# Post-norm layer on one core: in the setup, clip logarithms of chunks 1 and 2 on GpSimd, the third weight's scale and Wo's maxima sooner, ScalarE's queue reordered

## The chip, the cores and the metric
One core of one Trainium2 chip. The metric is the device time of one execution in microseconds (us).

## What is computed
The inputs are x (8 sequences of 2048 tokens, 256 features), four 256x256 matrices Wr, Wk, Wv, Wo, a decay and an ln weight of 256 values, and a feed-forward layer with 1024 hidden features. The reference, cut to what matters:

```
r = sigmoid(x @ Wr.T);  k = x @ Wk.T;  v = x @ Wv.T
dec = sigmoid(decay);   log_decay = log(clip(dec, 1e-7))
scale = exp(t * log_decay)                       # t = 0 .. 2047
cum = cumsum(k * v / clip(scale, 1e-10), axis=1)
y = rmsnorm(r * (cum * scale), ln_w)
x1 = layernorm(x + y @ Wo.T)
h = gelu(x1 @ (alpha1 * sign(w1)).T + b1)        # alpha = mean |w| of each row
out = layernorm(x1 + h @ (alpha2 * sign(w2)).T + b2)
```

## The kernel before
The tokens are cut into 32 chunks of 512 (4 to a sequence). A chunk passes through these steps: x is split into a high and a low half in fp16 (`xh` on ScalarE, `xl` on VectorE); TensorE forms k, v and r (`R`); VectorE multiplies them (`kvs`), where k is multiplied with a table `clip_g`; VectorE scans over time with the decay and multiplies by the gate (`scans`, result `y`); ScalarE forms the gate (`r_gates`) and the squares of y (`ysq`); GpSimd adds the squares and takes powers (`ysqs`, `y_scale`, `root_rms`); y is split (`yh`, `yl`), TensorE multiplies with Wo (`O`), VectorE adds the residual and normalizes (`residual1`, `ustats`, `norm1`). Then the first feed-forward layer (`F1`, `gelu`), the split of its result (`hh`, `hl`), the second one (`F2`), and the second norm.

The scan needs no exponentials, except where the reference's `clip(scale, 1e-10)` takes hold. That is what `clip_g` is for: for each feature and each time step in the sequence it holds min(1, exp(t * log_decay + 23.03)). It has 2048 columns, a part of 512 for each of the chunks 0 to 3 of a sequence, and is built once, in the setup. The parts 0 and 1 are built by `clip_logs(n)` on VectorE (t * log_decay, then the minimum with -23.03; two instructions, one for each half of the features) and `clip_table(n)` on ScalarE (exponential with a bias of 23.03, two instructions). The parts 2 and 3 are built by `clip_excess(n)` (a Relu) and `clip_table(n)` (exponential with scale -1), both on ScalarE.

Each engine works through a queue written by hand: a straight prologue, which fills the pipeline with chunks 0 to 3 and prepares the weights, and a loop over the chunks. Semaphores order the engines. The weights of k, v and r (numbered 0, 1, 2 in this order) are prepared one after the other: VectorE takes the maximum (`proj_maximum`), TensorE spreads it over the partitions (`sum_wmax`), VectorE makes the scale (`proj_scale`), ScalarE rounds the scaled matrix (`proj_split_hi`), VectorE makes its low half (`proj_split_lo`). The halved `w_inv` of the third one releases GpSimd's `unscales(0, 0)`, without which the first `kvs` can't start. Wo is prepared by `wo_maxima` (line 1133), `wo_scale`, `wo_split_hi`, `wo_split_lo`. `take_xbound(1, 1)` on VectorE (line 890) reads the sum that TensorE has formed from the squares of chunk 1's x (`xsq`, `sum_xbound`) and releases GpSimd's `scales(1, 1)` and `unscales(1, 1)`, and through them ScalarE's `xh(1)`. `signs` turns w1 and w2 into their signs, and the SP queue transposes these by DMA. `x1h(0)` (line 673) is the split of the first chunk's normalized rows, which TensorE has transposed in `T1(0)`; `x1l(0)` (line 992) is its low half; the first `F1` waits for it.

Of the kernel before, what the change touches and what calls it, by code (L numbers as in the profile page):

```python
# [27 lines left out]
def postln_layer_kernel(nc, x, Wr, Wk, Wv, Wo, decay, ln_w, w1, b1, w2, b2, out):  # L28
    fp32, fp16, bf16 = mybir.dt.float32, mybir.dt.float16, mybir.dt.bfloat16
    ALU, ACT, AX = mybir.AluOpType, mybir.ActivationFunctionType, mybir.AxisListType  # L30
# [23 lines left out]
    with ctx:  # L54
# [3 lines left out]
        def sem(name):  # L58
            return ctx.enter_context(nc.semaphore(name))
# [136 lines left out]
        s_w1T, s_w2T = sem("w1T_s"), sem("w2T_s")  # L196
        s_winv, s_wscl, s_proj_hi, s_alpha = sem("winv_s"), sem("wscl_s"), sem("proj_hi_s"), sem("alpha_s")
        s_clip, s_exp, s_nlog, s_excess = sem("clip_s"), sem("exp_s"), sem("neg_log_s"), sem("clip_excess_s")
        s_lnw, s_wo_hi = sem("lnw_s"), sem("wo_hi_s")
        s_passed = [sem("passed_pool_s"), sem("passed_dve_s")]  # L200

# [433 lines left out]
        def _(act):  # L635
# [100 lines left out]

            def clip_table(n):

                if n < 2:
                    act.wait_ge(s_clip, DC * n + DC)  # L740
                else:
                    act.wait_ge(s_excess, DC * n - DC)
                for dc in range(DC):
                    part = clip_g[:, dc, n * CH:(n + 1) * CH]
                    if n < 2:
                        nc.scalar.activation(part, part, ACT.Exp, bias=log_clip[:, :]).then_inc(s_exp, 1)
                    else:
                        nc.scalar.activation(part, part, ACT.Exp, scale=-1.0).then_inc(s_exp, 1)
# [33 lines left out]
            def prologue():  # L782
                xh(0, 0)
                proj_split_hi(0)
                clip_table(0)
                proj_split_hi(1)
                clip_table(1)
                proj_split_hi(2)
                xsq(1, 0, 1)
                clip_excess(2)  # L790
                r_gates(0, 0, (0,))
                clip_table(2)
                xh(1, 1, slot=1)
                signs(w1_in, w1_sgn, s_w1_in, s_sgn)
                xsq(2, 0, 2)
                r_gates(0, 0, (1,))
                wo_split_hi()
                ysq(0, (0,))
                ysq(0, (1,))
                r_gates(1, 1, (0,))  # L800
                clip_excess(3)
                yh(0)
                xh(2, 2, slot=2)
                clip_table(3)
                nc.scalar.activation(warm[:, :], ones_col[:, :], ACT.Gelu)
                r_gates(1, 1, (1,))
                signs(w2_in, w2_sgn, s_w2_in, s_sgn2)
                act.wait_ge(s_ysqs, 1)
                ysq(1, (0,), y=y_second)
                xsq(3, 0, 3, looped=True)  # L810
                alphas1()
                r_gates(2, 2, (0,))
                act.wait_ge(s_sgn2, 1)
                alphas2()
                x1h(0, 1)
                ysq(1, (1,), y=y_second)
                r_gates(2, 2, (1,))
                act.wait_ge(s_ready, 1)
                gelu(0, range(0, 1))
                yh(1, y_second)  # L820
                gelu(0, range(1, 2))
                act.wait_ge(s_ready, 2)
                hh(0, pairs[0])
                gelu(0, range(2, 4))
                hh(0, pairs[1])
                gelu(0, range(4, 6))
                hh(0, pairs[2])
                gelu(0, range(6, 8))
                x1h_rows(1, 1)
                hh(0, pairs[3])  # L830
                xh_rows(3, 3)
                take_alpha2_row()
# [47 lines left out]
        def _(dve):  # L880
# [239 lines left out]
            proj_scale(1)  # L1120
            proj_split_lo(0)
            proj_maximum(2)
            clip_logs(1)
            proj_split_lo(1)
            proj_scale(2)
            dve.wait_ge(s_wscl, 3)
            nc.vector.tensor_scalar_mul(w_inv[:, 2:3], w_inv[:, 2:3], 0.5).then_inc(s_winv, 1)
            proj_split_lo(2)

            def wo_maxima():  # L1130
                dve.wait_ge(s_wo_in, 16)
                dve.wait_ge(s_rows, 1)
                nc.vector.tensor_reduce(w_max[:, 3:4], wo_in[:, :, :], AX.XY, ALU.max,
                                        apply_absolute_value=True).then_inc(s_wmax, 1)
                nc.vector.tensor_reduce(w_max[:, 4:5], lnw_c[:, :], AX.X, ALU.max,
                                        apply_absolute_value=True).then_inc(s_wmax, 1)

            def wo_scale():

# [35 lines left out]

            def prologue():
                dve.wait_ge(s_exp, DC)
                kvs(0, 0, 0)
                take_xbound(1, 1)
                wo_maxima()  # L1180
                scans(0, 0, 0)
                xl(1, 1, slot=1)
                kvs(0, 0, 1)
# [92 lines left out]
        def _(pool):  # L1276
# [122 lines left out]
            nc.gpsimd.tensor_copy(fold[:, 1:TT, :], fold[:, 0:1, :].to_broadcast([P, TT - 1, P // TT]))  # L1399
            pool.wait_ge(s_setup_a, 2)  # L1400
            nc.gpsimd.tensor_scalar(neg_log[:, :], dec_c[:, 1, :], -1.0, 1.0, ALU.mult, ALU.mult).then_inc(s_nlog, 1)
            pool.wait_ge(s_winv, 1)
            unscales(0, 0)
            def prologue():
                scales(1, 1)
                unscales(1, 1)
                ysqs(0)
                y_scale(0)
                y_unscale(0)
# [70 lines left out]
```

## Time and profile before

| what | value |
|---|---|
| median of 3 runs | 821.02 us (820.99 to 821.21) |
| the profiled execution | 821.11 us, span 819.3 us |
| TensorE busy | 798.8 us, 97% of the span |
| VectorE busy | 771.3 us, 94% |
| ScalarE busy | 679.9 us, 83% |
| GpSimd busy | 295.3 us, 36% |

The span runs from the first to the last instruction. In the profile PE is TensorE, DVE is VectorE, ACT is ScalarE, POOL is GpSimd and SP is the queue that issues most DMAs. A busy share is an average over the whole span; the setup is its first 60 us or so.

### The profile page before, as it was taken

The page shows a single profiled execution, that of the slowest core. Times are in us where ns is not written, and L with a number is a line of the kernel's source. Part 1 is how long each engine was busy: PE and PEld are TensorE (multiplying, and loading weights), DVE is VectorE, ACT ScalarE, POOL GpSimd, SP SyncE. Part 2 cuts the span into 40 slices and gives each one's busy share as a digit, 9 for nine tenths or more (in the row PEclk, how much of TensorE's full clock was granted, in tenths as well). Part 3 has the DMA queues.
Part 4 walks back from the last instruction along what each step waited for, and adds up shares of the span by engine and source line. Part 5 has one row for each costly group of instructions (what it writes and reads, how often), then busy time and mean ns, then how long its engine had stood idle before and what let it go on. Part 6 is the DMA issues. An engine that isn't in the chain of part 4 may idle for free.

```text
span 819.3 us, 16575 instructions
## 1 busy us (share of the span) xinstructions
PE 798.8 (97%) x5174; PEld 505.7 (62%) x5174; DVE 771.3 (94%) x1472; ACT 679.9 (83%) x973; POOL 295.3 (36%) x572
## 2 busy tenths in 40 slices
PE   6989999999999999999999999999999999999986
PEld 4555666656666656666656666655666665666654
DVE  7998999999999999999999999999999999999887
ACT  7987888888888888888888888888888888887775
POOL 3343323344223344333344333344333334332344
PEclk9999999999999999999999999999999999999999
DMA  8513553434553434553434454444454344444313
GB/s 261 99 27 78 129 125 84 110 94 102 128 128 86 115 81 105 125 128 92 113 79 109 118 128 100 105 89 106 112 128 105 100 97 104 106 102 104 78 26 104
DMA packets 168286, 86.27 MB, mean 105 GB/s; under 512 B 128572, under 2 KB 163912, under 8 KB 168264
## 3 DMA queue, kind: packets, MB, share of 16 engines
q1 hardware_dynamic: 147288, 52.97, 27.5%
q0 software_dynamic: 4608, 16.78, 10.4%
q10 hardware_dynamic: 16368, 16.25, 5.6%
q8 instruction: 11, 0.18, 0.1%
q14 instruction: 11, 0.09, 0.0%
HBM read 20.45 MB, written 16.78 MB: 45 GB/s over the span
## 4 chain that ended last, share of the span: by engine, by line
PE 88%; DVE 4%; POOL 2%; ACT 2%; issue 2%; DMA 0%; SPq 0%; POOLq 0%; DVEq 0%; ACTq 0%
PE ps_r L375 28%; PE ps_o L496 26%; PE ps_f L446 19%; PE ps_r L446 6%; PE ps_o L401 6%; PE ps_o L406 3%; DVE hid_lo L1008 1%; DVE u L959 1%; ACT hid L678 1%; DVE u_st L967 0%; PE ps_s L383 0%; DMA x_in<-in_L_attn_x_dram 0%; POOL root L1322 0%; POOL y_sqs L1310 0%; DVE state L923 0%
## 5 line engine op out<-in xcount | busy, mean ns | idle before, releaser
L496 PE MATMUL ps_o<-w2T,hid_hi 128*128 128x256 f16 x992 | 218.9, 273 | 3.4 <-DVE hid_lo L1008 3.0
L496 PE MATMUL ps_o<-w2T,hid_lo 128*128 128x256 f16 x992 | 218.8, 272 | 0.0
L375 PE MATMUL ps_r<-x_t,proj_hi 128*128 128x512 f16 x768 | 197.1, 379 | 1.2 <-issue 0.7
L446 PE MATMUL ps_f<-x_t,w1T 128*128 128x512 f16 x768 | 181.7, 379 | 1.6 <-DVE x_t L992 1.3
L678 ACT ACTIVATE hid<-ps_f,rows_c,f_scale 128x512 f32<-128x512 f32 x192 | 145.2, 774 | 42.2 <-PE ps_f L446 37.1
L1008 DVE SCALAR_TENSOR_TENSOR hid_lo<-hid,hid_scale,hid_hi 128x1024 f16<-128x1024 f32 (+1 forms) x136 | 160.3, 1222 | 0.9 <-POOL hid_hi L1343 0.6
L1310 POOL TENSOR_TENSOR y_sqs<-y_sq 128x512 f32<-128x512 f32 x32 | 46.7, 1459 | 309.6 <-ACT y_sq L653 309.6
L375 PEld LDWEIGHTS ps_r<-x_t,proj_hi 128*128 128x128 f16 x768 | 74.7, 98 | 91.3 <-issue 2.8
L713 ACT ACTIVATE hid_hi<-hid,hid_scale 128x2048 f16<-128x2048 f32 (+2 forms) x72 | 127.9, 1778 | 3.2
L446 PEld LDWEIGHTS ps_f<-x_t,w1T 128*128 128x128 f16 x768 | 74.9, 98 | 79.7 <-issue 1.6
L375 PE MATMUL ps_r<-x_t,proj_lo 128*128 128x512 f16 x384 | 114.2, 379 | 0.2 <-DVE proj_lo L1084 0.2
L496 PEld LDWEIGHTS ps_o<-w2T,hid_hi 128*128 128x128 f16 x992 | 97.0, 98 | 20.2 <-DVE hid_lo L1008 5.9
L496 PEld LDWEIGHTS ps_o<-w2T,hid_lo 128*128 128x128 f16 x992 | 97.1, 98 | 14.4
L647 ACT ACTIVATE r_tanh<-ps_r,x_scl 128x512 f32<-128x512 f32 x64 | 43.9, 686 | 32.6 <-PE ps_r L375 29.4
L653 ACT ACTIVATE y_sq<-y 128x512 f32<-128x512 f32 x62 | 39.1, 630 | 37.0 <-ACT res L707 15.9
L446 PE MATMUL ps_r<-x_t,w1T 128*128 128x512 f16 x256 | 69.6, 378 | 0.0
L707 ACT ACTIVATE res<-res,z_shift,z_rstd 128x256 f32<-128x256 f32 x126 | 65.1, 589 | 4.8 <-POOL z_shift L1356 2.6
L1322 POOL TENSOR_TENSOR root<-ms,neg_half 128x4 f32<-128x4 f32 x32 | 32.8, 1024 | 93.0 <-DVE ms L949 93.0
L375 PEld LDWEIGHTS ps_r<-x_t,proj_lo 128*128 128x128 f16 x384 | 37.5, 98 | 45.7 <-DVE proj_lo L1084 0.9
L696 ACT ACTIVATE res<-u,u_shift,u_rstd 128x256 f32<-128x256 f32 x120 | 61.9, 588 | 1.7 <-POOL u_shift L1338 1.7
L923 DVE TENSOR_TENSOR_SCAN state<-decay_f,state,kvg 128x512 f32<-128x512 f32 x48 | 61.5, 1281 | 0.8
L401 PE MATMUL ps_o<-wo_lo,y_hi 128*128 128x256 f16 x248 | 59.2, 272 | 0.0
(191 smaller groups left out, 1332.2 us busy)
## 6 DMA issues: line engine op xcount, KB each, us to landing
x_in<-in_L_attn_x_dram SPq DMA_DIRECT2D x32, 512.0 KB, 4.1
res<-b_row POOLq DMA_DIRECT2D x32, 512.0 KB, 4.5
out_dram<-res ACTq DMA_DIRECT2D x31, 512.0 KB, 2.9
w_in<-in_L_ffn_w_dram SPq DMA_DIRECT2D x2, 1024.0 KB, 8.8
x_t<-x_st SPq DMA_TRANSPOSE x59, 3.7
b_row<-in_L_ffn_b_dram SPq DMA_DIRECT2D x1, 512.0 KB, 12.7
proj_in<-in_L_attn_Wk_dram SPq DMA_DIRECT2D x1, 256.0 KB, 3.8
proj_in<-in_L_attn_Wv_dram SPq DMA_DIRECT2D x1, 256.0 KB, 4.1
```

The lines of the kernel that those rows point to most:

```text
L375: last = nc.tensor.matmul(ps_r[:, m, :], w[:, m, dc, ec * P:(ec + 1) * P], xx[:, :, dc, :], start=(n == 0), stop=(n == 3 * DC - 1))
L401: nc.tensor.matmul(dst[:, tt, :], y_hi[:, dc, tt * P:(tt + 1) * P], w[:, dc, :], start=(dc == 0 and n == 0), stop=False)
L446: last = nc.tensor.matmul(f1_bank[hc % NF], w1T[:, hc, dc, :], xx[:, :, dc, :], start=(dc == 0 and n == 0), stop=(dc == DC - 1 and n == 1))
L496: last = nc.tensor.matmul(o_tok[:, tt, :], hh[:, hc, tt * P:(tt + 1) * P], w2T[:, :, hc, :], start=(hc == 0 and n == 0), stop=(hc == HC - ...
L647: nc.scalar.activation(r_tanh[:, ec, :], ps_r[:, 2, :], ACT.Tanh, scale=x_scl[:, j, 4:5]).then_inc(s_r, 1)
L678: nc.scalar.activation(hid[:, hc, :], f1_bank[hc % NF], ACT.Gelu, bias=b1c[:, hc:hc + 1], scale=f1_scale[:, hc:hc + 1]).then_inc(s_gelu, 1)
L696: nc.scalar.activation(res[j][:, tt, :], u[:, tt, :], ACT.Identity, bias=u_shift[:, tt:tt + 1], scale=u_rstd[:, tt:tt + 1]).then_inc(s_x1, 1)
L707: nc.scalar.activation(res[j][:, tt, :], res[j][:, tt, :], ACT.Identity, bias=z_shift[:, tt:tt + 1], scale=z_rstd[:, tt:tt + 1]).then_inc( ...
L713: nc.scalar.activation(hid_hi[:, part, :], hid[:, part, :], ACT.Copy, scale=hid_scale[:, :]).then_inc(s_hh, part.stop - part.start)
L923: nc.vector.tensor_tensor_scan(state[j % 2][:, ec, :], decay_f[:, ec, :], kvg[:, ec, :], first, ALU.mult, ALU.add).then_inc(s_scan, 1)
L1008: nc.vector.scalar_tensor_tensor(out=hid_lo[:, part, :], in0=hid[:, part, :], scalar=hid_scale[:, :], in1=hid_hi[:, part, :], op0=ALU.mult ...
L1310: nc.gpsimd.tensor_tensor(y_sqs[:, :], y_sq[:, 0, :], y_sq[:, 1, :], ALU.add).then_inc(s_ysqs, 1)
```

## The change
Five edits, all in the setup:
- the clip logarithms of chunks 1 and 2 are formed on GpSimd (`clip_logs_pool(1)` ahead of `unscales(0, 0)`, `clip_logs_pool(2)` behind `unscales(1, 1)`), with a semaphore of their own; `clip_logs(1)` leaves VectorE and `clip_excess(2)` leaves ScalarE, and `clip_table(2)` becomes an exponential with a bias;
- so the third weight's `proj_scale(2)` stands sooner in VectorE's queue;
- Wo's maxima stand ahead of `proj_split_lo(2)` and no longer behind `take_xbound(1, 1)`;
- `take_xbound(1, 1)` is put between k and v of the first `kvs`;
- in ScalarE's queue `clip_table(1)` and `clip_table(2)` are moved later, `clip_excess(3)` later as well (behind `xh(2)`), `xsq(2)` behind `wo_split_hi` and the first `ysq` ahead of it, behind `signs`.

```diff
@@ clip_table, ScalarE
-                if n < 2:
-                    act.wait_ge(s_clip, DC * n + DC)
+                if n == 0:
+                    act.wait_ge(s_clip, DC)
+                elif n < 3:
+                    act.wait_ge(s_clip_pool, DC * n)
                 else:
-                    act.wait_ge(s_excess, DC * n - DC)
+                    act.wait_ge(s_excess, DC)
                 for dc in range(DC):
                     part = clip_g[:, dc, n * CH:(n + 1) * CH]
-                    if n < 2:
+                    if n < 3:
                         nc.scalar.activation(part, part, ACT.Exp, bias=log_clip[:, :]).then_inc(s_exp, 1)
                     else:
                         nc.scalar.activation(part, part, ACT.Exp, scale=-1.0).then_inc(s_exp, 1)
@@ prologue, ScalarE
                 proj_split_hi(0)
                 clip_table(0)
                 proj_split_hi(1)
-                clip_table(1)
                 proj_split_hi(2)
                 xsq(1, 0, 1)
-                clip_excess(2)
                 r_gates(0, 0, (0,))
-                clip_table(2)
+                clip_table(1)
                 xh(1, 1, slot=1)
                 signs(w1_in, w1_sgn, s_w1_in, s_sgn)
-                xsq(2, 0, 2)
+                ysq(0, (0,))
                 r_gates(0, 0, (1,))
                 wo_split_hi()
-                ysq(0, (0,))
+                xsq(2, 0, 2)
                 ysq(0, (1,))
                 r_gates(1, 1, (0,))
-                clip_excess(3)
+                clip_table(2)
                 yh(0)
                 xh(2, 2, slot=2)
+                clip_excess(3)
                 clip_table(3)
@@ setup, VectorE
             proj_maximum(2)
-            clip_logs(1)
             proj_split_lo(1)
             proj_scale(2)
             dve.wait_ge(s_wscl, 3)
             nc.vector.tensor_scalar_mul(w_inv[:, 2:3], w_inv[:, 2:3], 0.5).then_inc(s_winv, 1)
-            proj_split_lo(2)
...
+            wo_maxima()
+            proj_split_lo(2)
@@ prologue, VectorE
                 dve.wait_ge(s_exp, DC)
-                kvs(0, 0, 0)
-                take_xbound(1, 1)
-                wo_maxima()
+                kvs(0, 0, 0, between=lambda: take_xbound(1, 1))
                 scans(0, 0, 0)
@@ setup and prologue, GpSimd
+            def clip_logs_pool(n):
+
+                pool.wait_ge(s_setup_a, 2)
+                part = slice(n * CH, (n + 1) * CH)
+                for dc in range(DC):
+                    nc.gpsimd.tensor_scalar(clip_g[:, dc, part], steps[:, part], dec_c[:, 1, dc:dc + 1], -LOG_CLIP,
+                                            ALU.mult, ALU.min).then_inc(s_clip_pool, 1)
+
+            clip_logs_pool(1)
             pool.wait_ge(s_winv, 1)
             unscales(0, 0)
             def prologue():
                 scales(1, 1)
                 unscales(1, 1)
+                clip_logs_pool(2)
                 ysqs(0)
```

## Rows read from the trace of the kernel before
**Rows 1.** Busy time by stretch; columns: length, each engine's busy us (instructions), clock, DMA.
```profile
0.00:63.10 63.10, 51.97 (x296) 30.67 (x296) 54.97 (x121) 53.69 (x92) 22.32 (x51) 1.00 0.49 126
63.10:774.80 711.70, 711.66 (x4636) 452.36 (x4637) 682.29 (x1276) 598.03 (x838) 253.25 (x490) 1.00 0.44 106
774.80:819.30 44.50, 35.14 (x244) 22.64 (x241) 34.09 (x77) 28.20 (x44) 19.71 (x31) 0.97 0.24 65
```
**Rows 2.** The chain that ended last, 12 to 19 us; columns: start, us, what.
```profile
12.17 0.80 DVE clip_g L1107 x2
12.99 0.94 ACT clip_g L746 x2
...
14.23 0.67 ACT proj_hi L726
...
18.03 1.24 DVE state L923
```
**Rows 3.** ScalarE in order of time, 17 to 44 us; columns: start, us, what.
```profile
17.25 0.67 ACT L647 ACTIVATE r_tanh<-ps_r,x_scl 128x512 f32<-128x512 f32 x1
17.82 1.14 ACT L748 ACTIVATE clip_g<-clip_g 128x512 f32<-128x512 f32 x2
...
23.73 0.84 ACT L754 ACTIVATE wo_hi<-ps_f,lnw_scl 128x256 f16<-128x256 f32 x2 [0.35 <-DVE lnw_scl L1146]
24.45 0.63 ACT L653 ACTIVATE y_sq<-y 128x512 f32<-128x512 f32 x1
...
25.52 0.63 ACT L653 ACTIVATE y_sq<-y 128x512 f32<-128x512 f32 x1 [0.34 <-DVE y L926]
...
26.81 1.51 ACT L734 ACTIVATE clip_g<-steps,neg_log_clip,neg_log 128x512 f32<-128x512 f32 x2
28.30 1.15 ACT L658 ACTIVATE y_hi<-y,y_roots 128x1024 f16<-128x1024 f32 x1
...
30.36 1.14 ACT L748 ACTIVATE clip_g<-clip_g 128x512 f32<-128x512 f32 x2
...
42.69 0.19 ACT L773 ACTIVATION_READ_ACCUMULATOR w_in<-w_in 128x1 f32 x1
43.12 1.02 ACT L673 ACTIVATE x_t<-ps_f 128x1024 f16<-128x1024 f32 x1 [0.24 <-PE ps_f L336]
```
**Rows 4.** VectorE in order of time, four places between 12 and 30 us.
```profile
12.87 0.74 DVE L1084 SCALAR_TENSOR_TENSOR proj_lo<-ps_o,w_scl,proj_hi 128x512 f16<-128x512 f32 x1
13.54 0.15 DVE L1079 TENSOR_SCALAR w_inv<-ps_s 128x1 f32<-128x1 f32 x1
13.72 0.16 DVE L1080 RECIPROCAL w_scl<-w_inv 128x1 f32<-128x1 f32 x1
...
17.18 0.68 DVE L1133 TENSOR_REDUCE w_max<-wo_in 128x1 f32<-128x512 f32 x1
...
28.46 1.30 DVE L923 TENSOR_TENSOR_SCAN state<-decay_f,state,kvg 128x512 f32<-128x512 f32 x1
```
**Rows 5.** GpSimd in order of time, three places between 4 and 30 us.
```profile
4.04 1.37 POOL L1395 TENSOR_SCALAR decay_f<-steps,dec_c 128x512 f32<-128x512 f32 x2 [0.43 <-DVE dec_c L1092]
...
27.56 0.71 POOL L1300 TENSOR_TENSOR y_roots<-y_q,halves 128x2 f32<-128x2 f32 x1
...
29.11 0.64 POOL L1285 TENSOR_TENSOR x_root<-x_scl 128x1 f32<-128x1 f32 x1
```
**Rows 6.** TensorE in order of time: the third product, and the first layer's.
```profile
15.00 1.02 PE L375 MATMUL ps_r<-x_t,proj_hi 128*128 128x512 f16 x4 [0.72 <-issue]
15.86 0.59 PE L375 MATMUL ps_r<-x_t,proj_lo 128*128 128x512 f16 x2
...
45.55 1.89 PE L446 MATMUL ps_f<-x_t,w1T 128*128 128x512 f16 x8 [0.56 <-DVE x_t L992]
```
**Rows 7.** Wo's load: its issue, and from the DMA view, median us to landing.
```profile
4.32 0.51 SPq L278 DMA_DIRECT2D wo_in<-in_L_attn_Wo_dram  x1
...
wo_in<-in_L_attn_Wo_dram SPq DMA_DIRECT2D x1, 256.0 KB, 5.7
```

More of the change, by code:

```diff
@@ L198, in postln_layer_kernel @@
         s_clip, s_exp, s_nlog, s_excess = sem("clip_s"), sem("exp_s"), sem("neg_log_s"), sem("clip_excess_s")
+        s_clip_pool = sem("clip_pool_s")
         s_lnw, s_wo_hi = sem("lnw_s"), sem("wo_hi_s")
```

## The prediction
> **What bounds the kernel now.** I read the busy table by stretches first [rows 1]. Of the span of 819.3 us the middle, from 63.1 to 774.8, has TensorE busy for 711.66 of 711.70 us at a granted clock of 1.00: there TensorE sets the pace and nothing in it can be shortened by a setup edit. The first 63.1 us have 51.97 us of TensorE, so 11.1 us of holes. All that this change touches lies there. A microsecond that the setup gives back moves the whole middle and the end by the same amount, if the state at 63.1 is only shifted.
>
> Then the chain of waits [rows 2]. In the setup it runs from VectorE's clip logarithms of chunk 1 (12.17, two of them, 0.80) to ScalarE's exponentials of them (12.99), because ScalarE has `clip_table(1)` in its queue ahead of the third weight's rounding (14.23), and then through ScalarE's `clip_excess(2)` to the first scan on VectorE (18.03).
>
> Last, ScalarE's order in time [rows 3]. The reader is to see two places. It waits for the scale of Wo (0.35 us before 23.73) and for TensorE ahead of `x1h(0)` (0.24 before 43.12). And from `yh(0)` at 28.30 to the end of the second alpha pass (42.69 + 0.19 = 42.88) it doesn't wait at all. It is full there, so what is put into this stretch is paid one for one, and what other engines gain ahead of it can't pass through it.
>
> **Part 1: the early shift.** Times below are those of before plus shifts.
> - VectorE no longer computes `clip_logs(1)`: 0.78 us (12.87 less 12.09) [rows 4]. `proj_split_lo(1)` starts at 12.09, and `w_inv` of the third weight comes not at 13.54 but at 12.09 + 0.67 = 12.76. The factor 0.67 is 13.54 less 12.87.
> - ScalarE no longer has `clip_table(1)` in front of `proj_split_hi(2)` (12.99 to 14.23) [rows 2]. The third weight's rounding waits for its scale only: the reciprocal starts 0.18 after `w_inv` and takes 0.16 [rows 4], with a hand-over of 0.04, so 12.76 + 0.38 = 13.14. That is 1.09 sooner.
> - TensorE's third product follows it from 15.00 to 13.91, and ends at 14.77 + 0.59 = 15.36, where before it was 16.45 [rows 6]. It needs the low half of this weight at 14.77: VectorE has `w_inv` halved by 13.3, Wo's maxima take 0.6 (0.68 from start to end [rows 4]) and about 0.1 for the small one, and Wo has been in SBUF since 10.0 (issued at 4.32, 5.7 to landing [rows 7]), so `proj_split_lo(2)` runs 13.95 to 14.69. It just fits. Moving `wo_maxima()` thus costs nothing here.
> - `kvs(0,0,0)`: k at 14.62 to 15.36. The bound of chunk 1 is read now between k and v. TensorE's sum for it stands right behind the third product, about 15.20 + 0.17, so VectorE reads it at 15.43 and v starts at 15.50. Without it v would start at 15.47. Price 0.03. Behind v the same read and Wo's maxima are gone.
> - First scan: v ends at 16.25, the gate (ScalarE at 15.45, since `clip_excess(2)` no longer stands before it) at 16.12, so the scan starts at 16.29 in place of 18.03 [rows 2]; y ends at 18.24.
> - ScalarE next: gate 15.45, `clip_table(1)` at 16.02 (0.57 later, as 17.25 to 17.82), 1.24 for it (12.99 to 14.23), `xh(1)` at 17.26 to 18.35. `xl(1)` on VectorE is at 18.38 where it was 20.00: **the shift is now 1.62 us**.
> - It stays so to `yh(0)`. VectorE's queue is the same from there on. ScalarE's moved `xsq(2)` now stands after the rounding of Wo. The factors of Wo come 1.62 sooner, ScalarE starts on Wo at 22.11, adds 0.72 (23.73 to 24.45) and 1.04 for the square, and is free at 23.87; the second `y` ends at about the same time (its square waited for it and started at 25.52 [rows 3]; less 1.62 that is 23.90). A tie: no loss, or 0.1. Then the sum of the bounds, GpSimd's `y_roots` (27.56 to 28.27 before [rows 5]) and `yh(0)` go from 28.30 to 26.68. `clip_table(2)`, 1.24, now fills 25.2 to 26.4, in the shadow of GpSimd's root where `clip_excess(3)` lay from 26.81 to 28.30.
>
> **Part 2: where it is given back.** `clip_excess(3)` is moved behind `xh(2)`, into the full stretch, and `clip_table(3)` waits for it directly. `yh(0)` 26.68, plus 2.06 for `yh` and `xh` (28.30 to 30.36), gives 28.74; plus 1.51 for the two excesses, and a hand-over of 0.02 to 0.1, gives 30.27 to 30.35 for `clip_table(3)`. Before it was 30.36. **Of 1.62 us there is 0.01 to 0.09 left on ScalarE.** TensorE and VectorE do arrive 1.62 sooner at `T1(0)`, but `x1h(0)` then waits for ScalarE. It used to wait 0.24 for TensorE after 42.88 (the next instruction may start 0.1 before the end of an accumulator read, so 0.34 of room). It starts at 42.78 less 0.01 to 0.09, that is 42.69 to 42.77, in place of 43.12: gain 0.35 to 0.43. I take 0.4.
>
> From there on everything hangs on `x1h(0)`: `x1l(0)` on VectorE and the first layer's product on TensorE, which waited for it until 45.55 [rows 6], then VectorE almost without a hole up to 63. So 0.4 arrives at 63.1, and the middle carries it to the end. The execution profiled took 821.11; the sum is 821.11 less 0.4, and the median of the runs shown is 0.09 lower, which gives 820.6.
>
> **Part 3: GpSimd.** It gets two pairs of 128x512 passes. The nearest row is the decay table of the same shape, 1.37 us for two [rows 5]. The first pair runs from 8.62 to 10.0, and what is queued behind it, `unscales(0,0)`, waits for `w_inv` until about 13.3 anyway: cover 3.3 us. The second stands after `unscales(1,1)` and before `ysqs(0)`, which is due at 24.7; it can start at 18.5 at the latest reckoning and end at 20: cover 4.7 us. Cost nothing, and if a pass took three times as long, the first pair would still end by 12.8. Its consumers come at 16.02 and 25.2.
>
> What the trace shows against it: GpSimd's `x_root`, one element per partition, takes 0.64 us (29.11 to 29.75), nearly as long as a pass over 512, and ends with VectorE's scan (28.46 to 29.76) [rows 4, 5]. So one of the two can stop the other. The Trainium skill ("SBUF — State Buffer", section "Who interferes with whom") makes it a lock: a VectorE instruction with two SBUF inputs and a GpSimd instruction that reads SBUF exclude each other for the whole instruction, and the first to start wins. By that rule, the row agrees, but it shows GpSimd as the loser only; this change could make VectorE the loser. By my schedule neither pair meets a scan or a y: the sum by the row and by the rule is the same unless the order slips.
>
> **The rivals.**
> - *A, the whole shift arrives*: ScalarE's full stretch gives way (a hole in it that I don't see, or the excess costs nothing there). The shift of 1.62 reaches `x1h(0)` as far as TensorE allows, 821.02 less 1.62 = 819.4. For it: TensorE and VectorE really are early. Against: [rows 3] has no hole between 28.30 and 42.88.
> - *B, slower: GpSimd's second pair takes the way of VectorE's first y.* `x_root` and the scan are both due at 16.3. If GpSimd gets in ahead of the y at 17.5 with both passes, y, `xl(1)`, and all up to `yh(0)` come 1.2 to 1.4 later than in part 1. Nothing absorbs it on the way, ScalarE is full behind it. Gain 0.4 less 1.3: 0.9 slower, 821.9. It decides once VectorE loses more than 0.4. Against: the y is in VectorE's queue before the passes can be, since two small operations precede them.
> - *C, the early shift is smaller than 1.62*: each 0.1 lost there is 0.1 lost at the end. Bounds: if only the 1.09 of the third weight comes through, the end is 0.1 slower, 821.2. The tie on ScalarE and the fit of the low half point this way.
> - *D, nothing is changed in the end*: the first layer waits for something else than `x1h(0)` (the transposed weights, say), 821.0. Their sign pass on ScalarE, from which they are transposed, comes 1.6 sooner as well, and in the trace the first layer waits for `x1l(0)` alone, 0.56 [rows 6].
>
> **How the numbers follow.** The forecast (gain of 0.2 to 0.6) 0.55, A and what lies between it and the forecast 0.12, B 0.08, C 0.15, D 0.10. The bound between a change and none is 0.2%, 1.64 us, so 819.38 to 822.66: the forecast, C, D and B all lie inside; A sits on the lower edge. Faster 0.08 (A with a bit more), same 0.89, slower 0.03 (B twice). The range: 819.7 holds all but the far half of A, 821.6 all but most of B.
>
> **What would show it.** The third weight's rounding near 13.1, the first scan near 16.3, `yh(0)` near 26.7: part 1. `clip_table(3)` within 0.1 of 30.3, no wait of ScalarE for TensorE ahead of `x1h(0)`, which starts near 42.7: part 2. GpSimd's four new passes 0.69 each, and no VectorE scan or y longer than 1.3 and 0.7: part 3. If `x1h(0)` starts near 41.5, A holds. If `xl(1)` starts after 19, B. The prediction is wrong if the middle stretch is no longer 711.7 us, for then the state at 63.1 is not merely shifted.

## The result and the profile after

The changed kernel takes 823.39 us (median of ten runs, 822.62 to 824.35), and the kernel before, run beside it, 821.11 (ten runs, 820.93 to 822.1). The ratio is 1.0027 with a 95% interval of 1.0019 to 1.0036: **slower by 0.27%, some 2.3 us**. Forecast were 820.6 and no measurable change. The profiled execution of the changed kernel took 824.16, with a span of 822.4.

The busy time of the changed kernel by stretch, cut at the same places of the program as [rows 1] (columns as there):

```profile
0.00:62.70 62.70, 51.93 (x294) 30.22 (x295) 52.54 (x117) 51.04 (x85) 31.51 (x55) 0.97 0.52 126
62.70:776.00 713.30, 712.01 (x4640) 452.16 (x4638) 682.30 (x1275) 598.94 (x841) 255.43 (x490) 1.00 0.44 105
776.00:822.40 46.40, 35.80 (x246) 22.71 (x243) 36.24 (x80) 28.69 (x46) 20.64 (x31) 0.95 0.28 78
```

Against [rows 1] three things stand out. TensorE's granted clock in the first stretch is 0.97 where it was 1.00. GpSimd (the fifth busy column) has 31.51 us there where it had 22.32. And the last stretch is 1.9 us longer, which no line of the diff touches. Both cuts are made by eye, so the middle's 713.3 and 711.7 can't be set against each other; GpSimd's sums of `y_sq` (`y_sqs` in the profile), one per chunk, tell the lateness better. The third, just behind the setup, is at 65.84 before and at 67.16 now (1.3 late); from the seventh to the last but one they are 1.38 to 1.42 late, in short 1.39; the last one (777.17 before) starts at 780.57, 3.4 late.

**The setup up to 27 us.** ScalarE and VectorE of the changed kernel in order of time:

```profile
13.18 0.69 ACT L727 ACTIVATE proj_hi<-ps_f,w_scl 128x512 f16<-128x512 f32 x1 [1.47 <-DVE w_scl L1082]
...
26.79 1.15 ACT L659 ACTIVATE y_hi<-y,y_roots 128x1024 f16<-128x1024 f32 x1 [0.19 <-POOL y_roots L1301]
...
28.63 1.11 ACT L640 ACTIVATE x_t<-ps_f,x_scl 128x1024 f16<-128x1024 f32 x1 [0.69 <-POOL x_scl L1281]
29.64 1.51 ACT L735 ACTIVATE clip_g<-steps,neg_log_clip,neg_log 128x512 f32<-128x512 f32 x2
31.18 1.15 ACT L751 ACTIVATE clip_g<-clip_g 128x512 f32<-128x512 f32 x2
...
43.62 1.00 ACT L674 ACTIVATE x_t<-ps_f 128x1024 f16<-128x1024 f32 x1
```
```profile
16.36 1.22 DVE L925 TENSOR_TENSOR_SCAN state<-decay_f,kvg 128x512 f32<-128x512 f32 x1
18.46 1.28 DVE L885 SCALAR_TENSOR_TENSOR x_t<-ps_o,x_scl,x_t 128x1024 f16<-128x1024 f32 x1 [0.15 <-ACT x_t L640]
...
26.92 1.28 DVE L925 TENSOR_TENSOR_SCAN state<-decay_f,state,kvg 128x512 f32<-128x512 f32 x1
```

Part 1 came to pass: the third weight's rounding at 13.18 (forecast 13.14), the first scan at 16.36 (16.29), `xl(1)` at 18.46 (18.38), `yh(0)` at 26.79 (26.68). Then `xh(2)`, the row at 28.63, waits 0.69 for a scale that GpSimd makes, and this makes `clip_table(3)` start at 31.18 (forecast 30.3) and `x1h(0)` at 43.62 (forecast 42.7, before 43.12 [rows 3]).

GpSimd of the changed kernel shows both the new passes and the late scale:

```profile
8.71 4.09 POOL L1409 TENSOR_SCALAR clip_g<-steps,dec_c 128x512 f32<-128x512 f32 x2
...
26.98 1.56 POOL L1281 TENSOR_TENSOR x_scl<-x_scl,neg_half 128x1 f32<-128x1 f32 x1
```

A pair of clip logarithms takes 4.09, three times the decay table's 1.37 [rows 5]. And `x_scl`, one element per partition, takes 1.56: it starts at 26.98, just inside VectorE's scan (26.92 to 28.20), and ends at 28.54, behind it. In e1, the changed kernel once more, the two lie almost the same way, and neither stops the other:

```profile
26.86 1.31 DVE L925 TENSOR_TENSOR_SCAN state<-decay_f,state,kvg 128x512 f32<-128x512 f32 x1
```
```profile
26.91 0.54 POOL L1281 TENSOR_TENSOR x_scl<-x_scl,neg_half 128x1 f32<-128x1 f32 x1
```

Here `x_scl` is done in 0.54, wholly inside the scan. It starts 0.05 behind the scan, and in after 0.06, so the profile's start times alone don't tell which of the two gets its turn.

**TensorE at 43 us** is where, in this trace, 0.5 us of lateness becomes 1.3. TensorE of the changed kernel in order of time:

```profile
43.07 0.17 PE L481 MATMUL ps_s<-w_max,ones 128*128 128x1 bf16 x1
45.29 0.18 PE L475 MATMUL ps_s<-bounds,ones 128*128 128x3 bf16 x1 [2.05 <-ACT y_sq L654]
46.02 3.54 PE L447 MATMUL ps_f<-x_t,w1T 128*128 128x512 f16 x8 [0.56 <-DVE x_t L994]
```
and the windows around it:
```profile
45.00:46.00 1.00, 0.18 (x1) 0.10 (x2) 1.00 (x4) 0.81 (x3) 0.69 (x1) 0.99 0.00 0
46.00:47.00 1.00, 0.97 (x3) 0.43 (x4) 0.93 (x7) 0.00 (x0) 1.00 (x2) 0.50 0.00 0
...
50.00:51.00 1.00, 1.00 (x10) 0.87 (x9) 1.00 (x1) 0.89 (x2) 0.00 (x0) 1.00 0.06 16
```

Before, TensorE stood at the same place as follows:
```profile
44.21 0.17 PE L480 MATMUL ps_s<-w_max,ones 128*128 128x1 bf16 x1
44.80 0.18 PE L474 MATMUL ps_s<-bounds,ones 128*128 128x3 bf16 x1 [0.42 <-ACT y_sq L653]
```

It worked until 44.38 and then had holes of 0.42 and 0.56. Now its work up to there ends 1.14 sooner, at 43.24, `x1h(0)` doesn't come sooner, and the holes are 2.05 and 0.56, with 0.18 of work between. The granted clock falls from 0.99 to 0.50, that is from 2.4 to 1.2 GHz, as the first layer starts, and its first eight products take 3.54 us where they took 1.89 [rows 6]. `x1h(0)` is 0.50 late and the loop 1.39, so 0.9 is added between them; in the traces of the experiments below in which ScalarE is late in the same way and the clock holds (e3, e4, e8, e9, e14) it is 0.04 to 0.08.

**The last chunk** has most of the rest. The chain of the changed kernel that ended last, from the statistics of the first chunk behind the loop (start, us, what):

```profile
765.36 0.20 POOL u_ve L1332
...
765.63 1.91 POOL u_rstd L1334
...
767.63 0.96 POOL u_neg L1336
...
768.75 1.03 POOL u_shift L1339
...
769.81 0.03 ACT res L697
```
In the same stretch of before the chain runs through TensorE alone, 16 us without a hole from 760.12 to 776.60. The same four GpSimd instructions of the kernel before, in order of time:
```profile
763.65 0.19 POOL L1331 TENSOR_SCALAR u_ve<-u_mv 128x4 f32<-128x4 f32 x1 [1.44 <-DVE u_mv L971]
763.92 1.01 POOL L1333 TENSOR_TENSOR u_rstd<-u_ve,neg_half 128x4 f32<-128x4 f32 x1
765.02 0.31 POOL L1335 TENSOR_SCALAR u_neg<-u_mv 128x4 f32<-128x4 f32 x1
765.81 0.20 POOL L1338 TENSOR_TENSOR u_shift<-u_neg,u_rstd 128x4 f32<-128x4 f32 x1 [0.48 <-POOL u_neg L1335]
```
and of the kernel after; then VectorE's `hid_lo` at that place, after and before:
```profile
765.36 0.19 POOL L1332 TENSOR_SCALAR u_ve<-u_mv 128x4 f32<-128x4 f32 x1 [1.76 <-DVE u_mv L973]
765.63 1.91 POOL L1334 TENSOR_TENSOR u_rstd<-u_ve,neg_half 128x4 f32<-128x4 f32 x1
...
768.73 1.05 POOL L1339 TENSOR_TENSOR u_shift<-u_neg,u_rstd 128x4 f32<-128x4 f32 x1 [0.15 <-POOL u_neg L1336]
```
```profile
765.39 1.28 DVE L1010 SCALAR_TENSOR_TENSOR hid_lo<-hid,hid_scale,hid_hi 128x1024 f16<-128x1024 f32 x1
```
```profile
764.00 1.27 DVE L1008 SCALAR_TENSOR_TENSOR hid_lo<-hid,hid_scale,hid_hi 128x1024 f16<-128x1024 f32 x1
```

From `u_ve` to the end of `u_shift` it is 2.36 before and 4.42 after, for the same four instructions. In idle time two places differ: before, there are 1.44 us ahead of `u_ve` and 0.48 ahead of `u_shift`; after, 1.76 and 0.15. It looks as if one pause of 0.33 had moved from the fourth instruction to the first. Behind it GpSimd comes too late for its turn against VectorE: before, `u_rstd` started at 763.92, 0.08 ahead of `hid_lo`, and took 1.01; now it starts at 765.63, inside `hid_lo` (765.39 to 766.67), and takes 1.91. The Trainium skill ("SBUF — State Buffer", section "Who interferes with whom") has this as an exclusive lock, held for a whole instruction and won by who starts first. Where GpSimd is the loser the trace agrees: `u_rstd` inside `hid_lo`, 1.91, and `x_scl` inside the scan, 1.56. Where it comes first the traces don't: before, `u_rstd` ran from 763.92 to 764.93, and `hid_lo`, started at 764.00, took its usual 1.27; in none of the sixteen traces does a `hid_lo` take over 1.29 (median 1.28) or a scan over 1.32 (median 1.28). The time is lost by GpSimd alone.

A smaller loss of the same kind is on VectorE, in the tail. The last pair of aggregates after, which waits 0.53 behind the statistics, and before, where no idle time is marked:
```profile
817.75 0.25 DVE L1045 BATCH_NORM_AGGREGATE z_mv<-z_st 128x2 f32<-128x6 f32 x2 [0.53 <-DVE z_st L1040]
```
```profile
814.71 0.25 DVE L1043 BATCH_NORM_AGGREGATE z_mv<-z_st 128x2 f32<-128x6 f32 x2
```

### The profile page after: what moved, and what is told of

Read it like the earlier page. It is cut to its first block, busy times and chain, and to the rows that moved or that the text cites. A ratio compares the mean times of both kernels' runs of the same rounds, so it can differ in the third digit from the quotient of the medians.

```text
span 822.4 us, 16574 instructions
## 1 busy us (share of the span) xinstructions
PE 799.7 (97%) x5174; PEld 505.1 (61%) x5174; DVE 771.1 (94%) x1470; ACT 678.7 (83%) x971; POOL 307.6 (37%) x576
## 4 chain that ended last, share of the span: by engine, by line
PE 85%; DVE 5%; ACT 4%; POOL 3%; issue 2%; DMA 0%; POOLq 0%; SPq 0%; DVEq 0%; ACTq 0%
PE ps_r L376 27%; PE ps_o L497 25%; PE ps_f L447 18%; PE ps_r L447 6%; PE ps_o L402 6%; PE ps_o L407 3%; DVE hid_lo L1010 1%; ACT hid L679 1%; DVE u L961 1%; DVE u_st L969 0%; POOL y_sqs L1311 0%; DMA x_in<-in_L_attn_x_dram 0%; PE ps_s L384 0%; POOL u_rstd L1334 0%; ACT w_in L769 0%
## 6 DMA issues: line engine op xcount, KB each, us to landing
b_row<-in_L_ffn_b_dram SPq DMA_DIRECT2D x1, 512.0 KB, 12.8
```

## The experiments

In each, "lateness in the loop" is that of GpSimd's sums of `y_sq` against before's trace (1.39 for the changed kernel), and medians are of 8 to 11 runs, but for e8 with its one; the kernel before, run on the same chip, stands behind them. The lowest and highest run are in brackets. The experiments were run in four groups, each on another chip: e1 to e4; e5 to e8; e9 to e12; e13 and e14. Across groups it is the differences to the kernel before that are compared.

**e1: the changed kernel again, and e8: what makes a pass on GpSimd long.** e1 has no edit. e8 leaves out the clipping:

```diff
-        ALU.mult, ALU.min
+        ALU.mult, ALU.add
```


> The changed kernel once more, nothing edited. It asks which of the holes seen in its first trace come back. Theory 1 (first layer held up by ScalarE, and then at half clock): x1h(0) again at 43.6, TensorE idle from 43.1 to 46.0 but for one small product, the first layer's first 8 products 3.5 us in place of 1.9, GpSimd's sums of squares of chunk 2 at 67.2, 1.3 behind before. Rival (all of it is scatter of single executions): some of these return to the values of before. The hold-up of 2.0 near 768 us, where the powers on GpSimd took 1.91 in place of 1.01, is expected to be scatter and to be gone: span 820.6 to 821.0. Time 822.5 to 824.3, 2.3 above before.

Measured: 823.64 (822.52 to 824.37), before 821.32, ratio 1.0026 (1.0017 to 1.0035). Its profiled execution took 822.57, with a span of 820.7: `xh(2)` does not wait, `x1h(0)` is at 42.74 as forecast, and the loop is 0.24 ahead of before. TensorE's holes ahead of the first layer are 1.62 and 0.56, and the granted clock falls again, but only in the middle of the first eight products (2.44, and 1.91 for the four behind them).

Yet its last sum of `y_sq` is 1.77 late, so the last chunk loses 2.0 again, by the same steps. What I had put down to scatter came back.

> The changed kernel with the minimum of GpSimd's clip passes replaced by an addition; it leaves out the clipping of the logarithms, so the tables of chunks 1 and 2 hold other values. Theory (the minimum is the slow operation): a pass takes 0.69 us like the decay table's multiply and add, in place of 2.05. Rival (it is the operands: a large steps array, or a scalar column and a constant): 2.05 as before. The time says little here, since the order of GpSimd's small operations under VectorE's scans changes too: 822.5 to 824.3 either way.

Measured: a pair takes 1.48 (0.74 each), so it is the minimum that makes a pass 2.05 long. The one run took 822.49 with a span of 820.7, as e1's profiled one (822.57, 820.7), and its last chunk loses 2.0 too, so the length of the passes isn't what makes the kernel slow. Its clock didn't fall, with TensorE's holes as in e1 (1.62 and 0.56). GpSimd of e8:

```profile
8.70 1.48 POOL L1409 TENSOR_SCALAR clip_g<-steps,dec_c 128x512 f32<-128x512 f32 x2
```

**e2: the excess put back early.** ScalarE's prologue:

```diff
 proj_split_hi(1)
+clip_excess(3)
 proj_split_hi(2)
 ...
 xh(2, 2, slot=2)
-clip_excess(3)
```


> The changed kernel with clip_excess(3) moved from behind xh(2) to ScalarE's hole of 1.47 us between the rounding of the second and of the third weight (11.7 to 13.2). Theory 1 (the excess in the full stretch of ScalarE is what delays the first layer, and the longer hole of TensorE ahead of it lets the clock drop): x1h(0) at 42.1 in place of 43.6, the hole of TensorE is about 1.3, no half clock, all later work 2.3 sooner than in the changed kernel: 820.1 to 820.6, as fast as before or 0.5 to 1 faster. Rival 2 (GpSimd's long passes are what costs): the rounding of the third weight is unchanged and the passes too, so the time stays at 823.4. Rival 3 (clock alone, independent of the excess): gain of the 1.5 only, 821.9.

Measured: 821.71 (821.23 to 823.62), before 821.32, ratio 1.0004 (0.9996 to 1.0013). The profiled execution is clouded: Wv landed late and VectorE waited 0.76 for it at 9.46, so `x1h(0)` came at 43.49, now with a wait of 0.24 for TensorE and not for ScalarE, and the clock held. The last chunk lost its 2.0. In the median it is 1.9 us faster than e1: the full stretch of ScalarE was the right place to look, and undoing it takes TensorE's long hole away too (0.43 is left).

**e3: TensorE kept at work in its hole.**

```diff
 sum_wmax(ps_wmax[:, 5:6], 5, 1, 6)
+pe.wait_ge(s_u, TT)
+idle_products(ps_o[:, 0, :], 16)
 sum_bounds(1, NCH)
+idle_products(ps_o[:, 0, :], 4)
```


> The changed kernel with 20 more idle products on TensorE (transposes of the identity into a bank that is free there), 16 ahead of the sum of chunk 1's bounds and 4 behind it, so that TensorE works through the hole of 43.1 to 46.0. x1h(0) stays at 43.6. Theory 1: the granted clock stays at 1.00 between 46 and 50, the first 8 products of the first layer take 1.9 and not 3.5, and of the 1.32 by which everything is late at 67 us only about 0.5 are left: 822.5. Rival (the half clock is hidden behind ScalarE and VectorE): no change in the time, 823.4.

The 20 products are transposes of the identity, and nothing reads them. Measured: 822.97 (822.37 to 824.96), before 821.32, ratio 1.0023 (1.0014 to 1.0031). The first layer's products took 1.89, so the clock held, but Wv was late again (0.78), and the last chunk lost its 2.0. Against e1 the median gains 0.7 and the lowest run 0.15; with single runs spread over 2.6 us that isn't clear of the scatter.

**e4: the scale ahead of the scan.** On GpSimd `y_unscale(0)` goes behind `unscales(2, 2)`:

```diff
-y_unscale(0)
 scales(2, 2)
 unscales(2, 2)
+y_unscale(0)
```


> The changed kernel with GpSimd's y_unscale(0) put behind unscales(2, 2), so that the power for chunk 2's scale starts at once behind y_roots at 26.8 and not behind VectorE's scan, under which it took 1.56 us. Theory 1: xh(2) no longer waits 0.69 but at most 0.1; the full stretch of ScalarE moves by 0.6, x1h(0) at 43.0 as before the change, the hole of TensorE 2.0 and not 2.6, and if that is short enough for the clock, 821.1; if not, 822.8. Rival (the chain ahead of x1h isn't what counts): 823.4.

Measured: 823.28 (822.44 to 824.96), before 821.32, ratio 1.0021 (1.0012 to 1.003). `xh(2)` has no wait, as it should, but in the profiled execution VectorE waited 0.32 for Wv, and TensorE's products from 11.82 to 14.38 took 1.91 and 1.06 where the changed kernel's took 1.03 and 0.60 (the granted clock is given as 1.00 there), so `x1h(0)` came at 44.79. TensorE's holes ahead of the first layer were 1.64 and 0.56, and the clock held all the same. The median moved by 0.4; the order of these two is not where the 2.3 us are.

**e5 and e6: only the position in GpSimd's stream.** The change gives GpSimd four instructions more. e5 puts four others, one spare element per partition each, into the kernel *before*; e6 puts four into the kernel *after*. Nothing reads them:

```diff
+for n in range(4):
+    nc.gpsimd.memset(spare[:, n:n + 1], -1.0)
 scales(0, 0)
```


> The kernel before with four more instructions on GpSimd, memsets of one spare column each, in a wait of the setup (5.4 to 7.4 us) where they cost nothing: as many as the change added to this engine. Theory (position in the code): where the first chunk behind the loop is worked off, GpSimd has one extra pause of 0.3 us at a fixed place of its instruction stream; four more instructions move it from ahead of u_shift (0.48 of idle in place of 0.15) to ahead of u_ve near 764 us, GpSimd then loses its turns against VectorE (u_rstd 1.91 and not 1.01, u_neg 0.95), and the end is 2.0 later: 823.2, as slow as the changed kernel, with the setup as before. Rival (the late loss comes from what the change does to the state of the loop, or is scatter): 821.1, u_rstd 1.01.

> The changed kernel with four such memsets more, so eight more instructions than before. Theory (position in the code): the pause moves on to an instruction ahead of u_ve, where GpSimd waits anyway, u_rstd near 764 takes 1.01, and the late loss of 2.0 is gone: 821.4, between -0.3 and +1.4 against the kernel before by what the setup did in that execution. Rival (the loss comes from the loop's state): 823.4, u_rstd 1.91.

Measured: e5 822.44 (822.23 to 823.43), before 821.12, ratio 1.0016 (1.0007 to 1.0025). The kernel before becomes 1.3 us slower by four instructions that nothing waits for, 0.21 us in all at 5.5 us of 820, ahead of a wait of 1.7. The loop isn't touched (0.03 ahead), the last sum of `y_sq` is 1.99 late. GpSimd of e5 at the place:

```profile
763.94 0.19 POOL L1332 TENSOR_SCALAR u_ve<-u_mv 128x4 f32<-128x4 f32 x1 [1.75 <-DVE u_mv L972]
764.22 1.90 POOL L1334 TENSOR_TENSOR u_rstd<-u_ve,neg_half 128x4 f32<-128x4 f32 x1
...
767.32 1.05 POOL L1339 TENSOR_TENSOR u_shift<-u_neg,u_rstd 128x4 f32<-128x4 f32 x1 [0.15 <-POOL u_neg L1336]
```

These are the rows of the changed kernel, to 0.01 us in what they take. e6: 822.16 (821.16 to 824.14), before 821.12, ratio 1.0009 (1.0 to 1.0018); it is 1.0 behind the kernel before where e1 is 2.3 behind, so four *more* instructions make the changed kernel 1.3 us faster, and `u_rstd` is back at 1.02. The pause depends on the position in GpSimd's instruction stream, and what stands there is hit.

**e7: the excess early, and four instructions more** (the edits of e2 and e6 together).

> Both mended: clip_excess(3) in ScalarE's early hole, and four memsets more on GpSimd. Theory: the 1.5 to 1.9 of the early excess and the 2.0 of the pause add up: 821.7 less 2.0 is 819.7, 0.2% faster than before. Rival (the two overlap, or the pause falls on another critical instruction): 821.7.

Measured: 820.17 (819.86 to 821.85), before 821.12, ratio 0.9994 (0.9985 to 1.0003). Against e6, on the same chip, the median gains 2.0. Here the early shift reaches the loop, 1.63 us of it, and the first layer's products take 1.89 from 43.88. ScalarE of e7, where `x1h(0)` waits for TensorE again:

```profile
41.46 1.02 ACT L675 ACTIVATE x_t<-ps_f 128x1024 f16<-128x1024 f32 x1 [0.24 <-PE ps_f L338]
```

**e9: the clock alone, with the pause out of the way** (e6 and the idle products of e3).

> The changed kernel with four memsets more on GpSimd (which took the late loss away) and the 20 idle products of TensorE ahead of the first layer. What is left of the change is then its setup at full clock. Theory 1 (the half clock ahead of the first layer is what spreads the executions of the changed kernel up): fewer executions above 822, median 821.0 where without the idle products it was 822.16. Rival (the spread comes from Wv's landing and from GpSimd's turns under VectorE's scan, which the idle products don't touch): the lowest stay at 821.1, the median stays near 822.

Measured: 821.33 (821.09 to 822.22), before 821.05, ratio 1.0003 (0.9994 to 1.0013). It is 0.3 behind the kernel before where e6 is 1.0 behind, so the median gains 0.8; the lowest run, 0.1 behind where e6's is 0.2, hardly moves. TensorE of e6, in whose trace the clock fell in the middle of the first layer (two windows behind: e6, then e9), and of e9:

```profile
45.24 2.36 PE L448 MATMUL ps_f<-x_t,w1T 128*128 128x512 f16 x8 [0.56 <-DVE x_t L995]
47.40 1.91 PE L448 MATMUL ps_r<-x_t,w1T 128*128 128x512 f16 x4
```
```profile
47.00:48.00 1.00, 1.00 (x4) 0.41 (x3) 0.97 (x3) 1.00 (x2) 0.90 (x3) 0.50 0.00 0
```
```profile
46.00:49.00 3.00, 2.34 (x14) 1.04 (x13) 2.97 (x4) 2.50 (x4) 2.32 (x5) 1.00 0.00 0
```
```profile
42.77 1.94 PE L459 MATMUL ps_o<-ident 128*128 128x128 f32 x16
...
45.26 1.89 PE L448 MATMUL ps_f<-x_t,w1T 128*128 128x512 f16 x8
```

The products of the first layer need 4.1 us at half clock in part (2.36 and 1.91, less the overlap) and 2.8 at full. The loop, though, is 0.15 ahead in e6 and 0.18 in e9: in these traces a fall in the middle of the layer was absorbed but for some 0.1 us. Where it came at the layer's start, as in the trace of after, it was not. That the median's 0.8 is the clock's isn't shown: the two were run on different chips, and on the chip of e6 more runs of the kernel before were slow too (8 of 27 above 821.6, on that of e9 2 of 29).

**e10 and e11: Wv made late on purpose.** x of chunk 1 is loaded between Wk and Wv, in the kernel before (e10) and in e6's (e11):

```diff
 load Wk
+load(1, 0, 1)
 load Wv
-load(1, 0, 1)
```


> The kernel before with chunk 1's x loaded between Wk and Wv, so that Wv, Wr land later on purpose, by 1 to 2 us, as happens by chance in some executions. Theory 1 (the setup before has room of its own for a late Wv, since clip logarithms and tables stand around it): the end moves by less than Wv does, 0.5 to 1.0, which is the upper group among the executions of before (821.6 to 822.4). Rival: the end moves as far as Wv, 822.5.

> The changed kernel with four memsets more on GpSimd and the same late Wv. Theory 1 (the change took the room out of the early chain and filled ScalarE's stretch behind it, so that a late Wv goes through to the first layer in full): x1h(0) 1.2 or more later than 42.8, the median 822.4 or more and the lowest above 822, farther from 821.2 than the kernel before moves with the same edit. Rival (both take it alike): the same step as in the kernel before.

Measured: e10 822.63 (821.94 to 824.31) and e11 823.64 (822.14 to 824.88), before 821.05, ratios 1.0023 (1.0014 to 1.0033) and 1.0031 (1.002 to 1.0041). VectorE waits 0.92 and 0.82 for Wv. The loop is 1.40 late in e10, and 2.03 later than e6 in e11, but the medians move alike, by 1.6 (e10 against before) and 1.5 (e11 against e6, each against its own before). The theory that the changed kernel pays more for a late Wv isn't shown. What is shown is that 0.9 us of waiting for one 256 KB load costs 1.4 us of the span in the kernel before. That both kernels' own scatter comes from this load is a guess that fits the traces of e2, e3, e4 and e13, in which it was late with no edit to it.

The wait isn't the whole price. In the traces of e2, e3, e4, e10 and e11 TensorE's products behind the late load also ran at about half their rate, until some time between 12.5 and 15.5 us (in e10 four took 1.91 from 12.33, before 1.03); the profile gives a granted clock of 1.00 for that stretch. In e13, with a wait of 0.42, they didn't, and its loop lost 0.5 against e7; in e4, with a wait of 0.32, they did, and its loop lost 2.0 against e1.

**e12: four instructions more again** (eight in the kernel before).

> The kernel before with eight memsets more on GpSimd, where four cost 1.3. Theory (a pause at a fixed place of the instruction stream): with eight it falls ahead of a wait that has room, u_rstd near 764 takes 1.01, time 821.1 as before. Rival (any added instruction costs, or the memsets cost in the setup): 822.4 or more.

Measured: 821.0 (820.95 to 821.54), before 821.05, ratio 0.9999 (0.999 to 1.0008). GpSimd of e12:

```profile
763.70 0.19 POOL L1332 TENSOR_SCALAR u_ve<-u_mv 128x4 f32<-128x4 f32 x1 [1.43 <-DVE u_mv L972]
...
765.54 0.20 POOL L1339 TENSOR_TENSOR u_shift<-u_neg,u_rstd 128x4 f32<-128x4 f32 x1 [0.15 <-POOL u_neg L1336]
```

The pause stands neither ahead of `u_ve` (1.43) nor ahead of `u_shift` (0.15, in before 0.48). With four instructions the kernel is 1.3 slower, with eight it is as it was: it is the place, not that there are more.

**e13 and e14: the same on VectorE.** The change takes two instructions off VectorE. e13 is e7, and e14 is e9, with two put back:

```diff
+for n in range(2):
+    nc.vector.memset(spare_v[:, n:n + 1], 0.0)
```


> The kernel with clip_excess(3) in ScalarE's early hole and four more memsets on GpSimd, and now also two memsets of spare columns on VectorE in its first wait (0 to 3.2 us), so that VectorE's stream is as long as before. Theory (VectorE has such a pause too, and the two instructions that the change removed pushed it ahead of the last bn_aggr): the idle before that one is 0.15 again and not 0.52, and the end comes 0.37 sooner than without them: span 817.7, lowest 819.5, median 819.8, 0.16% faster than before. Rival (the 0.37 belongs to something else in the tail): 820.2 as without them.

> The changed kernel with all three taken out: four memsets on GpSimd, two on VectorE, and the idle products of TensorE ahead of the first layer. What is left is the change's own effect in the setup, forecast as a gain of 0.4 (0.35 to 0.43). Theory: span 819.1, lowest 820.7, median 820.95 (0.37 less than the 821.33 without VectorE's two). Rival: 821.3.

Measured: e13 820.07 (819.49 to 821.67), before 821.11, ratio 0.9991 (0.9982 to 1.0); e14 820.97 (820.71 to 822.85), before 821.11, ratio 0.9999 (0.999 to 1.0008). The lowest run of e13 is 0.37 under that of e7, and the lowest of e14 is 0.38 under that of e9. VectorE's last aggregates in e6, without the two, and in e14, with them:

```profile
814.93 0.25 DVE L1046 BATCH_NORM_AGGREGATE z_mv<-z_st 128x2 f32<-128x6 f32 x2 [0.52 <-DVE z_st L1041]
```
```profile
814.41 0.25 DVE L1050 BATCH_NORM_AGGREGATE z_mv<-z_st 128x2 f32<-128x6 f32 x2
```

In e13's trace Wv was 0.42 late, and its loop is ahead by 1.12, not by 1.63. e13 is the fastest version found, 1.0 us below before in the median; its interval just touches 1. e14, the change with all three taken out, is 0.14 below before in the median, and its interval holds 1.

**The sum.** A span is that of before (819.3), plus the lateness in the loop, plus 1.3 where GpSimd's pause hits `u_ve` (2.0 at the last `y_sq`, of which the tail gives 0.7 back, by e5), plus 0.37 where VectorE's hits the aggregates. The 1.3 is taken from e5 and the 0.37 from the lowest runs of e7 and e13; the lateness is read from each trace, so the sum tests what lies behind the loop, not ahead of it:

```
kernel   sum                        measured span
after    819.3 +1.39 +1.3 +0.37 = 822.36   822.4
e1       819.3 -0.24 +1.3 +0.37 = 820.73   820.7
e2       819.3 +0.44 +1.3 +0.37 = 821.41   821.4
e5       819.3 -0.03 +1.3       = 820.57   820.6
e6       819.3 -0.15      +0.37 = 819.52   819.5
e7       819.3 -1.63      +0.37 = 818.04   818.1
e14      819.3 -0.29            = 819.01   819.0
```

The other eight traces fit as well as these, all within 0.1. The change also takes two instructions off ScalarE (973 to 971); no run puts them back, and the sum closes without them.

## Why the prediction was wrong

- **Part 1 was right.** Forecast against the trace: 13.14 and 13.18, 16.29 and 16.36, 18.38 and 18.46, 26.68 and 26.79. The tie on ScalarE held. Rival B didn't occur: VectorE's y was not held up. Of C there was 0.1: the shift at `yh(0)` was 1.51, not 1.62.
- **Part 2 was right in what ScalarE can pass on, where nothing else interferes.** In e1 `clip_table(3)` starts at 30.31 and `x1h(0)` at 42.74, inside the forecast 42.69 to 42.77, and with both pauses and the clock taken out of the way e14's loop is 0.29 ahead for the 0.4 forecast. In the profiled execution of after itself it failed by 0.9: GpSimd's power started 0.06 inside VectorE's scan and was held until its end. Part 3 wrote of such a pair "the row agrees, but it shows GpSimd as the loser only", looked for VectorE as the loser, which no trace shows, and left the scale's consumer, `xh(2)`, unpriced. Of the eight traces with this order and with the excess behind `xh(2)` only that one shows it, so it isn't the cause of the 2.3 us in the medians. Rival A was shut out by exactly the excess: with it moved (e7) the loop is 1.63 ahead.
- **Part 3's term was mis-sized.** 0.69 a pass was forecast, 2.05 measured, since the nearest row, the decay table's, has no minimum. The price was nothing all the same: the first pair ended at 12.80 and the second at 22.56, ahead of their readers, and e8, with passes of 0.74, is as slow as e1. The forecast's "if a pass took three times as long, the first pair would still end by 12.8" was what happened.
- **The step that failed** is "So 0.4 arrives at 63.1, and the middle carries it to the end", with its premise "if the state at 63.1 is only shifted". It failed twice. First, behind the loop: the time of the code there depends on where it lies in each engine's stream, and the change alters that by four GpSimd instructions and two VectorE ones. By e5, the first alone costs 1.3 us in the kernel before; by e1 and e6, 1.3 in the kernel after; the second costs 0.37 (lowest runs of e7 and e13, of e9 and e14). Second, ahead of the loop: an earlier `T1(0)` with an unmoved `x1h(0)` opens a hole on TensorE (0.42 before, 1.6 to 2.1 now), and the granted clock can fall: it did in after, e1, e6 and e11, and not in e4 and e8. In the trace of after the fall added 0.8 to the lateness, in e1 and e6 some 0.1; e6 and e9 differ by 0.8 in the median, which isn't shown to be the clock's. I had seen that TensorE and VectorE "arrive 1.62 sooner" and that `x1h(0)` would wait for ScalarE, and didn't ask what TensorE does meanwhile.
- **No rival named either place.** B, the one on the slow side, sought its loss on VectorE within the setup. The condition "wrong if the middle stretch is no longer 711.7 us" pointed to the right assumption, but at its harmless half: the loop ran in step, and the loss lay on both sides of it.
- Against the kernel before on the same chip, the medians of e1, e6, e9 and e14 are at +2.3, +1.0, +0.3 and -0.1. So of the 2.3 the first step, GpSimd's place, is 1.3; the next, with the idle products, 0.8; the third, VectorE's place, 0.4; and -0.1 is left for what the edit does by itself. The two places are shown by runs with and without the idle instructions and by their traces; of the middle step only the size is known.
- The forecast gain of 0.4 isn't confirmed either. With all three taken out (e14) it is 0.29 in the loop of one trace and 0.14 in the median, and the interval of its ratio holds 1.

What stays open: what the pause is. It keeps its place from trace to trace of one kernel, shows in straight code behind the loop and moves with instructions added before the loop; that it is the reading of instructions is a guess. Open too is why the clock falls behind a hole of 1.62 and 0.56 in e1, e6 and e11 and not in e4 and e8, and what the 0.8 between the medians of e6 and e9 is; one trace shows one execution, and where the clock falls it does so at another moment in each. Why products run at half rate behind a late Wv isn't known either. And how often GpSimd's power loses its turn at 26.9 can't be told from the few traces.

## What to carry to other kernels

An edit in the setup changes more than its own stretch: where two versions differ by a microsecond, count the instructions each engine has in each, and try the old kernel with as many idle ones before giving the edit the blame or the credit. An engine that is made earlier, without the one that it then waits for, only gets a hole, and for TensorE a hole can have a price of its own behind it (0.8 us in one trace, 0.1 or less in five). Move work out of the full stretch of the engine that is last, not into it: the same edit with `clip_excess(3)` left early gave 1.6 us at the loop instead of 0.2 to 0.3.

## What the runs showed of the hardware

- GpSimd: multiply and minimum over 128x512 f32 took 2.05 us, multiply and add 0.74.
- GpSimd and VectorE each showed a pause of 0.33 to 0.37 us in straight code behind a loop, at a place that moved with instructions added or taken out ahead of the loop. On GpSimd it cost four times its length at the end, as small instructions lost their turns against VectorE's: `u_rstd` 1.91 for 1.01, `u_neg` 0.95 for 0.31, `u_shift` 1.05 for 0.20.
- TensorE: after 2.05 and 0.56 us without work, with 0.18 between them, the granted clock was 0.50 (1.2 GHz) for some 3.5 us; eight products took 3.54 for 1.89. With 20 small products in the hole it stayed at 1.00 (three traces); with holes of 1.62 to 1.64 and 0.56 it fell in three traces and stayed in two.
- GpSimd against VectorE: `u_rstd` (normally 1.01) took 1.91 when it started 0.24 inside `hid_lo`; `hid_lo` took 1.27 when it started 0.08 behind `u_rstd`, as everywhere.
- The same load of a weight, 256 KB, made VectorE wait between nothing and 0.78 us in executions whose queues don't differ at that place. Behind waits of 0.32, 0.76 and 0.78 TensorE's products ran at about half their rate for 3 to 6 us, behind one of 0.42 they didn't.
